# Dense weights split beside the first dense products, ScalarE's tables loaded before the last dense rows, new orders behind the first and the last attention, and a shorter block table

## What is computed

```python
x = x + xattn(layernorm(x), ctx, ...)     # 16 heads (8 in layer 3), 77 keys for each of 4 sequences
x = x + ffn(layernorm(x), ...)
# layer 0: top 2 of 8 experts;  layers 1 and 3: top 1 of 8 experts
# layer 2 is dense:
h = silu(x @ w1.T * s1) * (x @ w2.T * s2)
h = gelu(h @ h1.T * s3)                   # h1, h2 are 512 x 512 with entries -1, 0, 1
h = gelu(h @ h2.T * s4)
out = h @ w3.T * s5
```

## Time and profile before

| | |
|---|---|
| median of 3 runs | 918.51 us (917.73 to 919.21) |
| profiled execution | 924.34 us, span 922.6 us |
| TensorE busy | 773.5 us, 84% |
| VectorE, ScalarE, GpSimd busy | 60%, 55%, 30% |
| mean granted TensorE clock | 0.937 of full |

### The profile page before, as it was taken

One profiled execution on the slowest core, in us unless ns is written; L12 is line 12 of the kernel. 1 busy time (PEld: TensorE's weight loads), 2 busy tenths in 40 slices (PEclk: granted clock), 3 DMA queues, 4 the chain that ended last, 5 costly groups with the idle time before them and its releaser, 6 DMA issues.

```text
span 922.6 us, 15702 instructions
## 1 busy us (share of the span) xinstructions
PE 773.5 (84%) x4631; PEld 612.8 (66%) x4631; DVE 557.1 (60%) x1967; ACT 505.5 (55%) x1662; POOL 277.7 (30%) x326
## 2 busy tenths in 40 slices
PE   3997978788887989989995999889999977757497
PEld 1575756657665667778973777738668855547497
DVE  4756646645447879655547887652232058984775
ACT  1876757235545987845644645464434255542275
POOL 4200023335550435433531434200010012342255
PEclk9999989869999999999997999999999998996599
DMA  7854694213225200002226920000000050000121
GB/s 228 221 174 183 155 217 119 71 48 85 82 63 218 70 1 13 10 17 68 60 78 193 210 55 1 1 0 1 1 1 0 1 183 1 1 12 13 45 69 48
DMA packets 35955, 69.57 MB, mean 75 GB/s; under 512 B 7120, under 2 KB 25808, under 8 KB 32032
## 3 DMA queue, kind: packets, MB, share of 16 engines
q1 hardware_dynamic: 30384, 57.98, 22.5%
q0 software_dynamic: 4768, 9.91, 3.1%
q10 hardware_dynamic: 720, 0.68, 0.2%
HBM read 58.45 MB, written 37.67 MB: 104 GB/s over the span
## 4 chain that ended last, share of the span: by engine, by line
PE 48%; DVE 22%; ACT 11%; issue 9%; POOL 6%; another core or an unknown queue 2%; DMA 1%; SPq 1%; DVEq 0%; POOLq 0%; ACTq 0%
PE bank L1156 9%; PE bank L1028 6%; PE bank L997 5%; PE bank L1131 4%; PE bank L956 3%; PE bank L1026 3%; PE bank L1011 3%; DVE s_xn L1309 3%; POOL out L2012 3%; ACT s_S L1820 2%; PE bank L1110 2%; PE bank L1104 2%; DVE s_peak L1346 2%; DVE s_total L1357 2%; POOL xs_L L2005 2%
## 5 line engine op out<-in xcount | busy, mean ns | idle before, releaser
L997 PE MATMUL bank<-s_A,s_xTq 128*128 128x462 f32 (+1 forms) x352 | 153.6, 528 | 23.8 <-DVE s_S L1343 11.6
L1978 POOL TENSOR_TENSOR s_S<-s_S,s_inv 128x462 f32<-128x462 f32 (+2 forms) x123 | 100.7, 837 | 167.8 <-DVE s_inv L1360 166.3
L1011 PE MATMUL bank<-s_ident,s_S 128*128 128x128 f32 (+2 forms) x560 | 91.0, 283 | 33.2 <-POOL s_S L1978 21.2
L1011 PEld LDWEIGHTS bank<-s_ident,s_S 128*128 128x128 f32 (+2 forms) x560 | 66.7, 143 | 76.8 <-POOL s_S L1978 35.7
L1843 ACT ACTIVATE s_PT<-bank 128x384 f32<-128x384 f32 (+1 forms) x176 | 81.7, 472 | 46.2 <-PE bank L1011 42.7
L1028 PE MATMUL bank<-s_VW,s_PT 128*128 128x128 f32 (+2 forms) x800 | 104.6, 288 | 1.9 <-DVE s_x L1390 1.9
L1028 PEld LDWEIGHTS bank<-s_VW,s_PT 128*128 128x128 f32 (+2 forms) x800 | 100.7, 204 | 6.7 <-DVE s_x L1390 3.4
L2005 POOL DMA_INDIRECT xs_L<-s_xn,s_sli x64 | 62.0, 969 | 115.1 <-DVE s_sli L1467 76.1
L997 PEld LDWEIGHTS bank<-s_A,s_xTq 128*128 128x128 f32 x352 | 57.6, 201 | 41.5 <-issue 13.5
L1811 ACT ACTIVATE s_S<-s_S 128x462 f32<-128x462 f32 (+1 forms) x80 | 45.3, 566 | 62.4 <-DVE s_S L1338 32.6
L1820 ACT ACTIVATE s_S<-s_S,s_peak 128x77 f32<-128x77 f32 x256 | 67.8, 351 | 7.6 <-DVE s_peak L1346 7.1
(11 more groups left out here) (235 smaller groups left out, 1672.1 us busy)
## 6 DMA issues: line engine op xcount, KB each, us to landing
xs_L<-xs_L SPq DMA_DIRECT2D x24, 1122.0 KB, 30.6
s_xe<-xs_L SPq DMA_DIRECT2D x85, 66.0 KB
s_moe<-in_L_w SPq DMA_DIRECT2D x2, 2048.0 KB, 10.6
s_moe<-in_L_w SPq DMA_DIRECT2D x8, 512.0 KB, 7.6
s_yb<-ys_L SPq DMA_DIRECT2D x12, 256.0 KB, 3.2
s_arena<-in_L_w SPq DMA_DIRECT2D x2, 1024.0 KB, 6.1
s_arena<-in_L_h SPq DMA_DIRECT2D x2, 1024.0 KB, 8.7
s_b2bc<-in_L_b SPq DMA_DIRECT2D x2, 512.0 KB, 24.5
```

Of the source, the lines that this page charges most:

```text
L997: mm(bank[b][:, 0:(h1 - h0) * KEYS], xTq_of(L, n)[:, i % 4, :], A[:, n, h0 * KEYS:h1 * KEYS], start=True, stop=True).then_inc(scores.up(L, ...
L1011: w = turn(bank[b][0:m, P * (t - t0):P * (t - t0) + P], S[s][:, P * t:P * t + m], ident)
L1978: p.tensor_tensor(val, val, rep(inv[s][:, h0:h1], KEYS, 2), ALU.mult).then_inc(normed.up(L, i, k), 1)
```

## The change

Five edits. The eight `split` pieces leave the side list of the third attention (layer 2): four follow the four `up` pieces of group 1, four the first four `mid` pieces. `tables` moves from behind the keys and values of layer 3 to ahead of the last eight `down` pieces. `finish(3)` has an order of its own. In `finish(0)` one `fold` of the next keys moves behind the tally. The block table is made in fewer steps, for all three expert layers: the number of blocks before each expert is summed directly through an overlapping view (`windows`), and one comparison table `past` gives both row and expert, where before two comparisons, three products and three shifted additions stood.

```diff
+        sent1 = [p for p in sides["after1"] if p[0] == "send"] if L == 3 else []
+        sides["after1"] = [p for p in sides["after1"] if p not in sent1]
         drain()
...
-                ("xt", "r", 0, 4), *steps("route", 4, 0), ("sigm", 0, 4), *keyed(4),
+                ("xt", "r", 0, 4), *steps("route", 4, 0), ("sigm", 0, 4), *keyed(3),
                 *steps("route", 4, 1, 2, 3, 4, 5, 6), ("sched", 0, 0), *steps("route", 4, 9), *steps("weigh", 4, 0, 1, 2),
...
+        elif L == 3:
+            choice, rest = upto(("route", 3, 2, 6), rest)
+            rows2 = [p for p in choice + rest if p[0] in ("ln", "own")]
+            choice = [p for p in choice if p[0] == "route"]
+            rest = [p for p in rest if p[0] in ("route", "weigh")]
+            now(("norm", 3, z, 0), *(("T", 3, z - 1, q) for q in nq), ("norm", 3, z, 1), *sent1, ("xt", "r", 3, 2),
+                ("O", 3, z - 2))
+            add(z - 2)
+            now(*rows2[:2], *norm("r", 3, 1), *(("T", 3, z, q) for q in nq), *norm("r", 3, 2), *rows2[2:3], *choice[:4],
+                ("O", 3, z - 1), *norm("r", 3, 3, 4, 5, 6, 7), *choice[4:], ("O", 3, z), ("xt", "r", 3, 3))
+            add(z - 1)
+            now(*rows2[3:])
+            add(z)
+            now(*norm("x", 3, 1), ("own", 3, 0), *norm("r", 4, 1, 2), *norm("x", 3, 2), *steps("route", 3, 0, 1),
+                *rest[:1], *norm("r", 4, 3, 4, 5, 6, 7), ("xt", "r", 3, 4), *rest[1:], *late, *steps("route", 4, 0),
...
+                *sends(3, 4), *(("sched", 3, st) for st in range(4, 7)))
+            return
...
-    side("split", [("split", n) for n in range(8)])
     attention(2)
...
     for g in (0, 1):
         for o in range(4):
             put("up", g, o)
+            if g:
+                put("split", o)
     for g in (0, 2):
         for h in (0, 1):
             for gg in (g, g + 1):
                 for o in range(4):
                     put("mid", h, gg, o)
+                    if h == gg == 0:
+                        put("split", 4 + o)
...
+        if g:
+            put("tables")
         for gg in (g, g + 1):
             for t in range(4):
                 put("down", 4 * gg + t)
...
-    put("tables")
     attention(3)
...
+    def windows(ap, first, n):
+
+        return bass.AP(ap.tensor, ap.offset + first, [list(ap.ap[0]), [1, n], [1, n]])
...
                 elif st == 3:
-                    dve.wait_ge(*filled.at())
-                    for n, e in enumerate((1, 2, 4)):
-                        again()
-                        v.tensor_tensor(cs[n + 1][:, 8:16], cs[n][:, 8:16], cs[n][:, 8 - e:16 - e],
-                                        ALU.add).then_inc(own.up(), 1)
+                    again()
+                    v.tensor_reduce(cs[1][:, 0:8], windows(cs[0], 1, 8), AX, ALU.add)
+                    v.tensor_scalar(tlf, cs[0][:, 8:16], -float(P), float(EROWS), ALU.mult,
+                                    ALU.add).then_inc(own.up(), 1)
                 elif st == 4:
                     again()
-                    v.tensor_tensor(a, rep(ij, 8, 2), rep(first, nbk, 1), ALU.is_ge)
-                    v.tensor_tensor(c, rep(ij, 8, 2), rep(cum, nbk, 1), ALU.is_lt)
-                    v.tensor_scalar(tlf, first, -128.0, float(-SPARE), ALU.mult, ALU.add).then_inc(own.up(), 1)
+                    v.tensor_tensor(past, rep(iotaj[:, 0:nbk], 8, 2), rep(cs[1][:, 0:8], nbk, 1),
+                                    ALU.is_ge).then_inc(own.up(), 1)
                     again()
-                    v.tensor_tensor(d, a, c, ALU.mult)
-                    v.tensor_tensor(cnt, tlf, ebase, ALU.add).then_inc(own.up(), 1)
+                    v.tensor_tensor(part[:, :, 0:8], past, rep(tlf, nbk, 1), ALU.mult).then_inc(own.up(), 1)
                     again()
-                    v.scalar_tensor_tensor(c, rep(ij, 8, 2), 128.0, rep(cnt, nbk, 1), ALU.mult,
-                                           ALU.add).then_inc(own.up(), 1)
-                    again()
-                    v.tensor_tensor(a, c, d, ALU.mult).then_inc(own.up(), 1)
-                    again()
-                    v.tensor_reduce(jf[1][:, 0:nbk], a, AX, ALU.add).then_inc(own.up(), 1)
+                    v.tensor_reduce(jf[1][:, 0:nbk], part, AX, ALU.add).then_inc(own.up(), 1)
```

More of the change, by code:

```diff
@@ L400, in finish @@
             add(z)
+        elif L == 3:
[13 more added lines that the diff above has]
+                *rest[:1], *norm("r", 4, 3, 4, 5, 6, 7), ("xt", "r", 3, 4), *rest[1:], *late, *steps("route", 4, 0),
+                *steps("route", 3, 2, 3, 4, 5, 6, 9), *steps("route", 4, 1), *steps("route", 3, 7),
+                *steps("route", 4, 2, 3), *norm("x", 3, 3, 4, 5, 7), ("own", 3, 1), *steps("weigh", 3, 0),
+                *steps("route", 4, 4, 5, 6), ("sched", 3, 0), *steps("route", 3, 10, 11), *norm("x", 4, 1), ("own", 4, 0),
+                *norm("x", 4, 2), *steps("weigh", 3, 1, 2), *steps("route", 3, 12), *sends(3, 3),
+                *steps("route", 4, 9), ("sched", 3, 1), ("sched", 3, 2), ("sched", 3, 3),
+                *norm("x", 4, 3, 4, 5, 7), ("own", 4, 1), *steps("weigh", 4, 0, 1, 2), *steps("route", 4, 10, 11, 12),
+                *sends(3, 4), *(("sched", 3, st) for st in range(4, 7)))
+            return
         else:
@@ L640, in body @@
     ysf = put("ysf", [P, 2, 4])
-    cnt = put("cnt", [P, 8])
     cmp16 = put("cmp16", [P, 8, 16])
-    cs = [put(f"cs{i}", [P, 16]) for i in range(4)]
-    jt = [put(f"jt{i}", [P, 39, 8]) for i in range(3)]
+    cs = [put(f"cs{i}", [P, 16]) for i in range(2)]
+    jt = [put(f"jt{i}", [P, 39, w]) for i, w in enumerate((8, 9))]
     jf = [put(f"jf{i}", [P, 39]) for i in range(2)]
@@ L1500, in vector_program @@
                 L, st = at
[L1501 to L1504, removed]
+                nbk = BLOCKS[L]
+                past, part = jt[0][:, 0:nbk, :], jt[1][:, 0:nbk, :]
                 if st == 0:
@@ L1510, in vector_program @@
                 elif st == 2:
+                    dve.wait_ge(*filled.at())
                     again()
@@ L1538, in vector_program @@
-                    again()
-                    v.tensor_reduce(jf[0][:, 0:nbk], a, AX, ALU.add).then_inc(own.up(), 1)
+                    v.tensor_scalar(jr[:, 0:nbk], jf[1][:, 0:nbk], float(SPARE), None,
+                                    ALU.min).then_inc(block_row.up(L), 1)
+                    v.tensor_reduce(jf[0][:, 0:nbk], past, AX, ALU.add).then_inc(own.up(), 1)
                 else:
                     again()
-                    v.tensor_copy(je[:, 0:nbk], jf[0][:, 0:nbk]).then_inc(block_expert.up(L), 1)
+                    v.tensor_scalar(je[:, 0:nbk], jf[0][:, 0:nbk], float(NE - 1), None,
+                                    ALU.min).then_inc(block_expert.up(L), 1)
```

3 lines of the change are left out of this document (1 added, 2 removed).

## The result

The changed kernel took 905.32 us (median of 5 runs, 904.41 to 910.79), the kernel before, measured again beside it, 919.21 us (5 runs, 917.73 to 924.39). The ratio is 0.9845, 95% interval 0.9819 to 0.9872: 1.55% faster, 13.9 us, where 12.4 us and 906.1 were predicted. The profiled executions took 924.34 us (span 922.6) and 910.79 us (span 909.1).

The account below looks back on a forecast made before the run. TensorE, busy 84% of the span, or the chain through it was taken as the bound. Splits 5.3, tables 2.7, layer 0 1.0 and last order 3.5 sum to 12.5 us, scaled 12.4: 906.1 us, range 901.5 to 911.

Parts of the forecast that it names:

- Splits out of the third attention: Third attention's start: 8.2 us won by the fifth clamp, 2.9 paid back later, net 5.3 us, bounds 2.3 and 7.3.
- 2 more, if TensorE's clock holds there: Third attention's start: upper bound, 2 us beyond the 8.2 if TensorE's clock stays up.
- (b): Rival: TensorE keeps its clock, perhaps 2 us more in the third attention and behind the last; 16.5 us, 902.1; chance 0.14.
- The lower bound: Third attention's start: only the eight VectorE subtractions count, 5.2 us, if ScalarE's part was covered anyway.
- The give-back: Gate stage: pieces with a split take 2.76 us instead of 2.12, making the first hidden product's fourth slice 2.9 us late.
- The term of 2.7: Behind the last dense products: two table loads removed, 2.56 us, and fold copies no longer late; 2.7, bounds 1.3 and 3.
- Layer 0 and the short table: Table alone 0 to 0.3 us in layer 0, 0 in layer 1; moved fold brings layer 0's block 1.0 us sooner.
- The order behind the last attention: Behind the last attention: layer 3's first block leaves 1.9 to 4.6 us sooner, 3.5 taken.
- 3.0 to 4.4: Behind the last attention: us of work moved past tile 15's addition, deducted from the 6.0 to 7.3 won.
- five steps of table and second norm ahead of the last slots (1.0): Behind the last attention: VectorE steps now behind tile 15's addition, charged 1.0 us before the last scatter.
- (a): Rival: less comes through, new last order gives nothing or third attention only its lower bound; 909.6 or 909.1; chance 0.20.
- (c): Rival: late splits idle TensorE at the dense products' head, clock falls to 1.2 GHz; 920 to 925 us; chance 0.03.

Follow-up runs that it names:

- e9_copies: The changed kernel with ScalarE's eight split copies back in the third attention, VectorE's subtractions left in the gate stage; ratio to the kernel before 0.9842.
- e5_inside4: The changed kernel with splits 0 to 3 issued inside the gate pieces of group 1 instead of behind them; 876.65 us, ratio to the kernel before 0.9835.
- e2_tables: The kernel before with only the preload of ScalarE's table moved ahead of the last dense rows; ratio 0.9979.
- e1_splits: The kernel before with only the eight weight splits moved from the third attention to the gate stage and first hidden products; ratio 0.9914.
- e3_order3: The kernel before with only the new order behind the last attention, old block table kept; ratio 0.9950.
- e10_scatters_first: The changed kernel with GpSimd's four scatters of group 1 again ahead of the small product of tile 15; ratio to the kernel before 0.9908.
- e6_inside8: The changed kernel with all eight splits inside the gate pieces, one in each; 874.34 us, ratio to the kernel before 0.9812.
- e0_after: The changed kernel unedited, measured again as a yardstick; 879.76 us, ratio to the kernel before 0.9863.
- e4_table: The kernel before with only the short block table, in all three routed layers; ratio 1.0000.

## Why the prediction was right, and where it was not

The total came within 0.8 us, but partly by luck: the kernel before measured 0.7 us slower than in the sum, and errors cancel. Against the sum, the profiles gave 2.5 us more at the splits and 1.7 more at the last order, but 0.6 less at the tables, 2.0 less up to layer 0's first block and 0.6 less at the end. Both large terms came out above their own upper bounds (7.8 against 7.3, 5.2 against 4.6).

**Splits out of the third attention.** The 8.2 us up to the fifth clamp were 8.43, and they came through whole. The step that failed is the one that left the clock out of the sum: "2 more, if TensorE's clock holds there" stood as an upper bound and in rival (b), and was there, 2.2 us of the 10.63, though 1.6 of it went in a dip 55 us behind the first score that no term had. The page on the clock gate says that idle gaps between bursts drop the clock (the Trainium skill, "TensorE: Matmul & The Clock Gate", HAM oscillation); I weighed it only against the gate stage, while it spoke for taking the gaps out of the attention. The lower bound was wrong in kind: it priced VectorE's subtractions by their busy time, 5.2 us, and `e9_copies` shows that 8.4 hang on them.

**The give-back.** 2.9 predicted, 2.85 measured, for the reason given: the piece with a split took 2.66 us (2.76 in the sum), and the fourth slice came 2.74 us late against the gate products. The term was right as a price of that place, but `e5_inside4` shows that the work itself is free there. Splits 4 to 7 cost nothing, as said.

**Tables.** The term of 2.7 was over-sized; it measured 2.08. Two loads of 1.28 went from the chain, and the copies of the folds behind them are no second gain on top, as the sum had it, but the way in which the loads cost time. Before, TensorE waited for such a copy in the middle of its folds:

```profile
746.13 1.82 PE L956 MATMUL bank<-s_ctxT,s_GM 128*128 128x308 f32 x6 [1.80 <-ACT s_A L1751]
```

From the first fold to the turning of the query rows it took 747.79 - 741.48 = 6.31 us; after the change, without that wait, 738.86 - 734.61 = 4.25. That is 2.06 of the 2.08; the other 0.5 of the two loads did not come through. The page's price (the Trainium skill, "ScalarE: Activation LUTs", What ACT_TABLE_LOAD costs) would have made it 5.3, which `e2_tables` rules out; in the profile the operation behind each of the two loads starts within 0.02 us of the load's end.

**Layer 0 and the short table.** 0.76 and 0.93 us in two profiles for the 1.0, layer 1 nothing (its first block comes 220.61 us behind layer 0's before and 220.59 after), layer 3 0.3. In the profiled pair it was hidden by 1.7 us that the execution of the changed kernel had lost by layer 0's last gate products (187.31 against 185.60).

**The order behind the last attention.** The mechanism held: against the scores, which came 8.94 us sooner, the addition of tile 15 is at 836.25 + 8.94 = 845.19, for which 845.2 was predicted. The step that failed is the count of what went behind that addition, "3.0 to 4.4". It was 15.97 us from there to the last scatter instead of 13.51, 2.5 more. All of it stands ahead of the scatter that waits for group 3's slots (`s_sli`); there one VectorE wait for an exponential is 1.00. From that scatter on, GpSimd issues its last five 1.26 us apart in both kernels, before and after:

```profile
860.96 0.96 POOL L2005 DMA_INDIRECT xs_L<-s_xn,s_sli  x1 [5.28 <-DVE s_sli L1467]
...
847.17 0.96 POOL L2029 DMA_INDIRECT xs_L<-s_xn,s_sli  x1 [1.52 <-DVE s_sli L1500]
```

The last scatter starts 5.06 and 5.05 us behind these. The slots of group 4, the last, are ready 0.9 us ahead of their first scatter (850.03 against 850.96). So the "five steps of table and second norm ahead of the last slots (1.0)" stand beside GpSimd's scatters and cost nothing: the sum charged them to a stretch that GpSimd paces. Without them the count is 2.0 to 3.4, and the 2.5 lies in it. So the part gave 5.2 us where 3.5 stood.

**The end.** Nothing was predicted there; this pair of profiles lost 0.60 us. In the first 8 us behind the block TensorE had 0.52 of full clock instead of 0.61. But the kernels with the old order differ among themselves in this stretch, 53.6 to 55.4 us, so that the change costs anything there is not shown.

**Rivals.** (a) is out by `e1_splits` and `e3_order3`. (b) came true in the third attention. Behind the last one TensorE was at full clock up to the addition of tile 15, which the sum's 845.2 holds already, and at 0.50 from 839 us on, as before from 841; what the clock gave there beyond the sum can't be told apart. (c) did not come: 1.00 through the dense products in every profile, although TensorE idled 1.54 us as forecast. Two profiles have a dip at the head of the gate stage; it cost 1.1 us in `e10_scatters_first` and nothing that can be seen in `e6_inside8`.

## What to carry to other kernels

Work that is moved out of a chain of two engines that answer each other was here best put inside another such chain, in the gap in which each waits for the other's answer, and not between its pieces: the same splits cost 8.4 us in one place (10.6 with the clock), 2.85 behind the gate pieces, and nothing inside them. Price a step on a strictly ordered engine by what it waits for and by what stands behind it, not by its busy time. Where TensorE waits and its clock is low, taking out the waits can give back more than they last (2.2 us beside 8.4 here, and not all of it at the same place). Where two engines stand behind one another at the end of a stretch, look which of them paces it before steps are charged to the other. And a move that removes a gap of one engine (here a small product ahead of four scatters) may be worth most of a long reordering.

## What was unexpected in the hardware

- **TensorE's clock differs between executions in code that is the same.** From 85 to 100 us, in layer 0's attention, it had 0.94 before and 0.79 after, and 0.78 in `e0_after`, 0.98 in `e6_inside8`, 1.00 in `e4_table`. The additions of tiles 4 and 5 there are 8.8 us apart at the higher clock (88.72 and 97.49 before) and 10.4 at the lower (90.16 and 100.55 after). Such dips move the total by 2 to 3 us, more than the smaller terms of this sum. Whether some kernels draw them more often than others, as the medians of `e5_inside4` and `e6_inside8` may suggest, stays open.
- **Two levels of the whole run.** The same kernel took 892 and 923 us in different groups of runs. From layer 0's first block to layer 1's it was 203 us against 220.6, and SyncE's loads of layer 0's blocks spread over 41.6 us against 53.3, while the stretches from the third attention on agree within 2 us where the code is the same. Both levels stand on record for one and the same chip, in different groups of runs, so the chip alone does not make them. The cause was not looked for.
